# A two-layer conv/attention kernel: the next batch's normalised input staged through DRAM, and the maximum products placed at other points of the score loop

## The reference

```
xn = group_norm(x, 32 groups) * gamma + beta        # per image
q, k, v = split(w_qkv @ xn + b_qkv)                  # 8 heads of 64 channels, 1024 positions
weight = softmax((q*s)^T (k*s), over the keys), s = 64**-0.25
a = weight @ v
out = x + w_proj @ a + b_proj
```

## Time and profile before

| | us |
|---|---|
| median of 3 runs | 2838.94 |
| the runs | 2837.18 to 2839.82 |
| the profiled execution | 2841.34 |
| its span on the core | 2839.8 |
| TensorE matmuls busy | 2620.9 (92%) |
| VectorE busy | 1653.4 (58%) |
| GpSimd busy | 1139.3 (40%) |
| ScalarE busy | 988.6 (35%) |

### The profile page before, as it was taken

The page is one execution under the profiler, slowest core; times in us unless marked ns, Lnnn a source line. Parts: engine busy times, 40 slices in busy tenths (PEclk is TensorE's granted clock), DMA queues, the critical chain, the costliest instruction groups (busy, mean ns, idle before and its releaser), DMA issues.

```text
span 2839.8 us, 38561 instructions
## 1 busy us (share of the span) xinstructions
PE 2620.9 (92%) x13908; PEld 1728.6 (61%) x13908; DVE 1653.4 (58%) x1757; ACT 988.6 (35%) x1215; POOL 1139.3 (40%) x522
## 2 busy tenths in 40 slices
PE   8999999998998999899899989998999899899988
PEld 6888788886554655465447545654655465457544
DVE  5545455455567547745764676367547745764655
ACT  3232222222234323423442343234324423442433
POOL 3320000000264445635661765264445635661762
PEclk9999999998999999999999999999999999999999
DMA  5331111112001110121012011201110121012001
GB/s 182 127 114 40 45 48 44 59 60 96 23 23 39 52 68 23 52 86 42 8 45 104 23 38 45 75 23 40 50 68 23 52 89 39 9 44 104 16 15 60
DMA packets 59262, 155.58 MB, mean 55 GB/s; under 512 B 8704, under 2 KB 8704, under 8 KB 59136
## 3 DMA queue, kind: packets, MB, share of 16 engines
q1 hardware_dynamic: 55552, 141.07, 14.1%
q0 software_dynamic: 3584, 12.58, 1.3%
HBM read 111.69 MB, written 41.94 MB: 54 GB/s over the span
## 4 chain that ended last, share of the span: by engine, by line
PE 79%; DVE 10%; issue 4%; ACT 3%; POOL 3%; DMA 1%; DVEq 0%; ACTq 0%; POOLq 0%; SPq 0%
PE psum L1062 17%; PE psum L1244 13%; PE psum L1293 12%; PE psum L1279 12%; PE psum L1081 6%; PE psum L1254 5%; PE psum L1105 4%; DVE small L901 3%; PE psum L1133 3%; POOL a_all L494 3%; PE psum L1307 2%; DVE r_all L884 2%; PE psum L1176 2%; ACT a_all L648 1%; DVE r_all L892 1%
## 5 line engine op out<-in xcount | busy, mean ns | idle before, releaser
L494 POOL TENSOR_TENSOR a_all<-a_all 128x1024 f32<-128x1024 f32 x441 | 1072.9, 2433 | 1050.0 <-ACT a_all L648 1017.1
L901 DVE TENSOR_REDUCE small<-psum 128x2 f32<-128x1024 f32 x512 | 627.0, 1225 | 426.6 <-PE psum L1254 426.6
L648 ACT ACTIVATE a_all<-psum 128x1024 f32<-128x1024 f32 x512 | 496.1, 1021 | 479.4 <-PE psum L1279 479.4
L1279 PE MATMUL psum<-r_all 64*128 64x512 f32 x4096 | 524.4, 394 | 13.9 <-ACT a_all L648 11.3
L1293 PE MATMUL psum<-a_all 128*64 128x512 f32 x2048 | 499.8, 614 | 9.6 <-ACT a_all L648 7.6
L1062 PE MATMUL psum<-r_all 128*128 128x512 f32 x1920 | 459.2, 400 | 15.6 <-DVE small L901 9.8
L1279 PEld LDWEIGHTS psum<-r_all 64*128 64x128 f32 x4096 | 383.8, 186 | 116.5 <-ACT a_all L648 39.7
L1062 PEld LDWEIGHTS psum<-r_all 128*128 128x128 f32 x1920 | 368.3, 193 | 105.6 <-DVE small L901 12.0
L1244 PE MATMUL psum<-r_all 128*128 128x512 f32 x1536 | 369.2, 396 | 55.9 <-DVE small L901 33.6
L1244 PEld LDWEIGHTS psum<-r_all 128*128 128x128 f32 x1536 | 284.2, 188 | 146.1 <-DVE small L901 37.6
L1254 PE MATMUL psum<-r_all 64*128 64x512 f32 x1024 | 237.7, 459 | 92.2 <-DVE r_all L892 49.1
(11 more groups left out here) (115 smaller groups left out, 1779.4 us busy)
## 6 DMA issues: line engine op xcount, KB each, us to landing
r_all<-w_dram SPq DMA_DIRECT2D x48, 1024.0 KB, 5.1
a_all<-y_dram SPq DMA_DIRECT2D x9, 2048.0 KB, 7.9
a_all<-x SPq DMA_DIRECT2D x16, 1024.0 KB, 6.6
y_dram<-a_all SPq DMA_DIRECT2D x16, 1024.0 KB, 4.2
out<-a_all SPq DMA_DIRECT2D x32, 512.0 KB, 3.0
a_all<-y_dram SPq DMA_DIRECT2D x56, 256.0 KB, 2.7
w_dram<-r_all POOLq DMA_DIRECT2D x16, 512.0 KB, 3.0
a_all<-w POOLq DMA_DIRECT2D x16, 256.0 KB, 3.0
```

Of the source, the lines that this page charges most:

```text
L494: pool.tensor_tensor(p_sum[:, :, cols], probs[:, 0, :, cols] if i == 1 else p_sum[:, :, cols], probs[:, i % SLOTS, :, cols], ALU.add).then ...
L648: act.activation(probs[:, i % SLOTS, :, cols], psum[half][:, :, :], ACT.Exp, scale=SCALE).then_inc(probs_ready, 1)
L901: dve.reduce_max(max2[:, :, tile, half], psum[3][:, :, :], AX_X).then_inc(work_free, 2)
L1279: last = pe.matmul(psum[half][:, h], k[rows_], q[rows_], start=(t == 0), stop=(t == 3))
```

## The change

It does four things. (1) The input of batch b+2 is normalised and split in the tail of batch b (units 0 to 3 beside the V tiles, 4 to 7 beside the projections), stored from a third of `probs` to a DRAM tensor `xn_dram`, and loaded whole into `xn` in one transfer of 4 MB in p = 2 of batch b+1. Batch 1's is staged in the opening phase, beside the first V tiles. ScalarE's queue issues the stores and the later loads of `y_half`. (2) Normalising stands between the reciprocals and behind the last Q/K tile; `hid_lo` follows maxima 0 and 1, and `hid_hi` stands before the last Q/K tile and behind the first exponentials. (3) The maximum products have new places: one behind every score tile, one between the two halves of score tiles 1, 3, 5, 6 and 7, one behind the weighings that follow tiles 1, 3 and 5. None is left before the first score tile or behind the last weighing. (4) Weighings come after the odd score tiles only: 0, then 1 and 2, then 3 and 4, then 5, 6 and 7. The loops over b now end at B - 2, and the last two batches are written out.

```diff
@@ -265,8 +269,13 @@
...
-        NORM_STEP = (1, 2, 3, 3, 4, 5, 5, 6)
-        LO_AT = (4, 6, 8, 9, 10, 12, 13, 14)
+        UNITS = NH * CT
+        EARLY = UNITS // 2
+
+        def unit(u):
+            return u // NH, slice(u % NH * HALF, (u % NH + 1) * HALF)
+
+        MID = (1, 3, 5, NT - 2, NT - 1)
@@ -389,22 +397,25 @@
...
+            load_y(1)
...
-                    load_y(b + 1, range(2))
-                if not last:
-                    load_y(b + 1, range(2, NH * CT))
+                if stage:
+                    load_y(b + 2)
...
                 if not last:
+
+                    for half in xn_stored:
+                        sp.wait_ge(half, (b + 1) * (UNITS // 2) * 16)
+                    sp.dma_start(f(xn), f(xn_dram[b + 1])).then_inc(xn_loaded, 16)
@@ -568,18 +580,36 @@
...
+            def store_xn(tb, u):
+
+                j, cols = unit(u)
+                act.wait_ge(xn_lo_done, tb * UNITS + u + 1)
+                act.dma_start(f(xn_dram[tb, :, :, j, cols]), f(stage_r[:, u % 2])).then_inc(xn_stored[u % 2], 16)
+                if u + 2 < UNITS:
+                    j, cols = unit(u + 2)
+                    act.dma_start(y_half[:, u % 2], y_v[tb, :, j, cols]).then_inc(y_half_loaded[u % 2], 16)
+
+            def norm_unit(tb, u, scale, bias):
+
+                made = (tb - 1) * (UNITS // 2) + u // 2
+                act.wait_ge(y_half_loaded[u % 2], (made + 1) * 16)
+                act.activation(y_half[:, u % 2], y_half[:, u % 2], ACT.Identity, scale=scale(u // NH),
+                               bias=bias(u // NH)).then_inc(xn_made, 1)
+                act.wait_ge(xn_made, tb * UNITS + u + 1)
+                if u >= 2:
+
+                    act.wait_ge(xn_stored[u % 2], made * 16)
+                act.activation(stage_r[:, u % 2, HI], y_half[:, u % 2], ACT.Copy).then_inc(xn_hi_done, 1)
+                if u:
+                    store_xn(tb, u - 1)
+                if u == UNITS - 1:
+                    store_xn(tb, u)
@@ -601,21 +631,24 @@
...
             for i in range(NT):
...
                 act.activation(v_t[:, i], bank(i % CT), ACT.Copy).then_inc(v_first_done, 1)
...
+                norm_unit(1, i, lambda j: xn_scale[:, j, 1:2], lambda j: xn_bias[:, j, 1:2])
...
                     for i in range(QK):
+                        if more and p and i == QK - 1:
+                            hid_hi(b, p - 1, 0)
                         if more:
                             qk_hi((p + 1) % PAIRS, par, i)
@@ -647,16 +684,10 @@
...
                             act.activation(probs[:, i % SLOTS, :, cols], psum[half][:, :, :], ACT.Exp,
                                            scale=SCALE).then_inc(probs_ready, 1)
-                        if p and i in (2, 3):
+                        if p and more and i == 0:
+                            hid_hi(b, p - 1, 1)
+                        if p and not more and i in (2, 3):
                             hid_hi(b, p - 1, i - 2)
-                        if p == 2 and not last:
-                            if i == 1:
-
-                                act.wait_ge(work_full, qk_used(b, 2))
-                                act.wait_ge(next_norm_ready, 2 * b + 2)
-                            for u in range(NH * CT):
-                                if NORM_STEP[u] == i:
-                                    norm_half(b + 1, u)
...
+
+                def stage_units(us_):
+                    for u in us_:
+                        norm_unit(b + 2, u, lambda j: next_norm[:, 0, j:j + 1], lambda j: next_norm[:, 1, j:j + 1])
+
+                if stage:
+
+                    act.wait_ge(sum_step, ONE + (b * PAIRS + PAIRS - 1) * ADDS + 2 * (2 * SLOTS - 1))
+                    act.wait_ge(next_norm_ready, 2 * b + 2)
+                    stage_units(range(EARLY))
                 for h in range(NH):
                     hid_hi(b, PAIRS - 1, h)
@@ -878,10 +922,9 @@
...
-            def norm_lo(b, u):
-                j, cols = u // NH, slice(u % NH * HALF, (u % NH + 1) * HALF)
-                dve.wait_ge(xn_hi_done, b * NH * CT + u + 1)
-                dve.tensor_tensor(xn[:, LO, j, cols], y_half[:, u % 2], f(xn[:, HI, j, cols]), ALU.subtract).then_inc(xn_lo_done, 1)
+            def norm_lo(tb, u):
+                dve.wait_ge(xn_hi_done, tb * UNITS + u + 1)
+                dve.tensor_tensor(stage_r[:, u % 2, LO], y_half[:, u % 2], f(stage_r[:, u % 2, HI]), ALU.subtract).then_inc(xn_lo_done, 1)
@@ -976,9 +1019,11 @@
...
+                if m % 2:
+                    norm_lo(1, m // 2)
             max_join()
@@ -994,36 +1039,27 @@
...
                         invert_sums(pairs - 1, 1)
                     next_qk(2)
                     next_qk(3)
-
-                    def between(m):
-                        if p:
-                            if m in (0, 1):
-                                normalise(pairs - 1, m)
-                            if m in (6, 8):
-                                hid_lo(b, p - 1, (m - 6) // 2)
-                        if p == 1 and m == 4 and not last:
-
-                            dve.wait_ge(xn_hi_done, (b + 1) * NH * CT)
-                            for i, of in enumerate((xn_scale, xn_bias)):
-                                dve.tensor_copy(next_norm[:, i], of[:, :, bass.ds(b + 1, 1)].rearrange("p j a -> p (j a)")).then_inc(next_norm_ready, 1)
-                        if p == 2 and not last:
-                            for u in range(NH * CT):
-                                if LO_AT[u] == m:
-                                    norm_lo(b + 1, u)
+                    if p:
+                        normalise(pairs - 1, 1)
 
                     if more:
                         if p == 0:
                             dve.wait_ge(max_ready, pairs + 1)
                         for m in range(MAXES):
                             max_tile(m)
-                            between(m)
+                            if p and m < NH:
+                                hid_lo(b, p - 1, m)
+                            if p == 1 and m == 4 and stage:
+
+                                dve.wait_ge(xn_hi_done, (b + 2) * UNITS)
+                                for i, of in enumerate((xn_scale, xn_bias)):
+                                    dve.tensor_copy(next_norm[:, i], of[:, :, bass.ds(b + 2, 1)].rearrange("p j a -> p (j a)")).then_inc(next_norm_ready, 1)
                         max_join()
                     else:
-                        for m in range(2):
-                            normalise(pairs - 1, m)
                         for i in range(1, NT):
                             add_last(i, pairs)
                             if i in (4, 5):
@@ -1037,22 +1073,27 @@
...
                         v_tile(b + 1, i)
+                        if stage and i < EARLY:
+                            norm_lo(b + 2, i)
                         if i in (1, 2):
                             invert_sums(pairs, i - 1)
                         if i in (3, 4):
                             normalise(pairs, i - 3)
                         if i in (5, 6):
                             hid_lo(b, PAIRS - 1, i - 5)
-                for o, half in proj_tiles(last):
+                for t, (o, half) in enumerate(proj_tiles(last)):
                     n, ps = work.next()
...
-
-            with dve.Fori(0, B - 1) as b:
...
+                    if stage and 2 <= t < 2 + UNITS - EARLY:
+                        norm_lo(b + 2, EARLY + t - 2)
+
@@ -1264,7 +1305,7 @@
...
-            def scores(pairs, par, i):
+            def scores(pairs, par, i, between):
                 keys = slice(i * P, (i + 1) * P)
@@ -1278,6 +1319,8 @@
...
                     last.then_inc(scores_full, 1)
+                    if half == 0 and i in MID:
+                        between()
@@ -1352,14 +1395,18 @@
...
-                                    pe.wait_ge(xn_lo_done, (b + 2) * NH * CT)
+                                    pe.wait_ge(xn_loaded, (b + 1) * 16)
...
-                    def next_max(m):
+                    made = [0]
+
+                    def next_max():
+                        m = made[0]
+                        made[0] += 1
                         if more:
-                            if m < 2:
-
-                                pe.wait_ge(qk_hi_done, (pairs + 1) * QK + 3 + m)
+                            if m == 0:
+
+                                pe.wait_ge(qk_hi_done, (pairs + 2) * QK)
                             max_tile(1 - par, m)
 
@@ -1368,19 +1415,19 @@
...
-                    next_max(0)
 
                     pe.wait_ge(work_free, turned)
-                    scores(pairs, par, 0)
-                    next_max(1)
-                    for i in range(1, NT):
-                        scores(pairs, par, i)
-                        next_max(2 * i)
-                        weigh(b, p, i - 1)
-                        if i < NT - 1:
-                            next_max(2 * i + 1)
+                    for i in range(NT):
```

(57 more changed lines are left out.)

24 lines of the change are left out of this document (13 added, 11 removed).

## The result

| | before | changed |
|---|---|---|
| median, us | 2839.4 (2837.2 to 2843.7) | 2914.1 (2907.7 to 2919.6) |
| ratio | | 1.0258, interval 1.0235 to 1.0280 |
| the profiled execution | 2841.3 | 2907.7 |
| its span | 2839.8 | 2906.0 |

The change costs 75 us in the medians (four executions of each kernel), 66 in the profiled executions. I had forecast +34, in a range of my own of 2855 to 2895; the wide range, 2836 to 2915, takes the median in by 1 us, at the end that rival D had set. The lines have moved: the maximum product is L1295 now and its reduction L944, scores L1320, weighings L1336, Q/K tiles L1285, V and projection tiles L1103, the addition that evacuates a projection tile L1089; in the staging L602 scales a unit, L927 makes its lower part, L593 stores it and L596 asks for the y of the unit after the next.

The account below looks back on a forecast made before the run. TensorE was taken to bound the kernel, four fifths of the chain of waits. Terms 20 + 27.3 + 7.8 + 19 - 43.4 + 7.5 - 4 gave +34, so 2873 us; own range 2855 to 2895, wide range 2836 to 2915.

Parts of the forecast that it names:

- rival D: Batch tails: the staging chain ends late, last unit some 3.4 us after its bank is wanted; 2908 us, chance 0.12.
- p = 0: +20: First pair of each batch: new order makes the score part 41.0 us instead of 38.5, +2.5 us, 8 times.
- The round of 1.89 us: Score loop: next maximum waits for the reduction, 1.89 us from the last maximum to next work, binding the short gaps.
- rival A: Score loop: the maximum's round is shorter than assumed, so the change is faster; 2814 us at 1.70, chance 0.12.
- The +1.4 of the second lower half: Score loop: hid_lo(1) waits for GpSimd's running addition and delays the fourth maximum, +1.4 us in each of 23 pairs.
- rival B: Score loop: hid_lo(1) slips in ahead of GpSimd's first addition, -1.4 x 23, giving 2841 us; chance 0.08.
- p = 1 and later: Later pairs: p=3 +27.3, last batch's p=1 and p=2 +7.8, other p=1 +19, p=2 without normalising -43.4 us.
- The staging's tail term: Batch tails: a lower part delays a value tile's evacuation 0.5 us, 6 times, +3 us (bounds 0 and 20).
- where I had 4.5: Opening phase: ScalarE and VectorE go at the staging chain's pace from the third unit, +4.5 us (bounds 2 and 17).
- where 7.5 stood: Whole moved staging, opening and tails, with the 4 MB reload hidden: +7.5 us in all.
- 4.8 us a unit: Staging chain: 0.81 to scale, some 0.6 copy, 0.7 for two issues, 2.7 to landing, 4.8 us per unit.
- Rival C: Score loop: short gaps in series lower TensorE's clock, 1.6 us for each of 31 series; 2923 us, chance 0.08.

Follow-up runs that it names:

- run 5: Changed kernel with key tiles weighed singly and a maximum behind every score product and every weighing but the last, only tile 1's halves apart: 2821.7 us, 0.9931.
- run 3: Changed kernel with GpSimd's first addition of a pair waiting until the previous pair's hid_lo is written: 2891.7 us, 1.0196.
- run 9: Changed kernel with the lower parts of units 4 to 7 behind projection tiles 0, 1, 3, 5 instead of 2, 3, 4, 5: 2902.7 us, 1.0214.
- run 7: Changed kernel with each unit's store and the following load issued ahead of the next unit, so two loads are under way: 2909.3 us, 1.0242.
- run 10: Changed kernel with late lower parts behind projection tiles 0, 1, 3, 5, and store and reload issued ahead of the next unit: 2868.8 us, 1.0100.
- run 6: Changed kernel with each load of y issued ahead of the previous unit's store on ScalarE's queue: 2900.5 us, 1.0213.
- run 2: Kernel before with only the new order of maximum products and weighings: 2954.5 us, 1.0420.
- run 1: Changed kernel with the old order of maxima and weighings, keeping the staging and the moved normalising and hid_lo: 2837.8 us, 0.9989.
- run 11: Changed kernel with a maximum behind every score product and weighing but the last, three early and five late units, loads ahead of stores and next unit: 2758.3 us, 0.9702.
- run 12: Old order of maxima and weighings with three early and five late staged units, loads ahead of stores and of the next unit: 2780.3 us, 0.9792.

## Where the prediction held and where it failed

Direction, place and mechanism of the order's cost were right; the sum was 32 us short in the profiled executions, nearly all of it in one term.

**The pairs** came out within 0.8 us of the working. p = 0: +20 on record (54.0 us each), 53.9 to 54.2 us where its first tile ran at full pace. The round of 1.89 us is there and rival A is out (run 5 shows from the other side that the short gaps are the cost: with about 2 us of work between maxima the pair is 51.7). The +1.4 of the second lower half is confirmed by run 3, which takes 1.2 of it away in p = 2 and 3, and rival B is out. This is what the Trainium skill's page "SBUF — State Buffer", section "Who interferes with whom", states of the shared port: a VectorE instruction with two SBUF inputs and a GpSimd instruction that reads SBUF shut each other out. The durations 2.46 beside GpSimd and 0.74 behind the gate agree. p = 1 and later were sized some 0.2 to 0.8 us a pair too high, about 9 us in all.

**The staging's tail term failed.** On record it was 0.5 x 6 = +3, from "the later units end with projection tiles 5 and 6, before the bank is needed". Measured, the six staged tails are 52.2, 52.1, 52.1, 51.2, 51.5 and 49.8 us against 46.8: +28. The first pairs behind them are 2.2 to 3.8 us longer than 54.0, but for the last: +15. The loop's very first pair is +1.5, and the opening window of the earlier trace rows +5.6, where I had 4.5. Together 50 us stand where 7.5 stood, +42; less the 9 us above, that is about the 32 that were missing. Rival D named this mechanism, at 3.4 us a tail and a chance of 0.12; it is 4.7 us a tail and the clock on top.

Three things made the chain slower than 4.8 us a unit. I let a unit start when its inputs were there, and overlooked that unit 6's load hangs on unit 4's lower part, which VectorE's program places behind projection tile 2: it is made 7.5 us after its upper half (995.5 to 1003.0), of which the chain loses some 3, since ScalarE has unit 5 until 1001.0. I took the landing from a trace in which these loads had no stores in their queue, 2.7 us; behind a 512 KB store it is 3.4 to 8.7, median 3.9:
```profile
DMA to landing us min/median/max: 3.4/3.9/8.7
```
And the weights and stores of the result fall into the same stretch. Run 9 shows that the place alone is worth 11 us, run 7 that the second load alone is worth 5 at most, run 10 that both together are worth 45: each cause hides the other. Of the last load's 7.4 us its own queue's store is the smaller part, for with the load ahead of it (run 6, 14 us in all) the load still took 6.5 to 7.8, and with the store ahead of it but the weights behind (run 10) 4.4. The larger part goes with the weights in front of it.

**Rival C**, the clock, was wrong where I had placed it: ten short gaps a pair leave the granted clock at 1.00 (p = 1 to 3 above). The rule of the Trainium skill, "TensorE: Matmul & The Clock Gate", section "A second HAM failure mode: psum-queue depth-cycling", which has the clock swing where TensorE idles briefly between many groups, did not show in these pairs. The rival holds for the long wait ahead of a batch: the stretch behind it is granted 0.96 (0.94 to 0.96 in five of six), and its first tile takes 4.6 to 5.5 us in five of six.

**What the parts are worth.** The new order costs 113 us on the kernel before (run 2) and 76 on the staged one (run 1 against the changed kernel). The staging is worth nothing under the old order as it stands, for its tail eats the 10 us a batch that p = 2 gives back, and 57 us once it is spread.

## What to carry over

Where work is moved into another stage, write down for each transfer which instruction of which engine must be over before it is *issued*, at its place in that engine's program; the chain of these, not the sum of durations, set here when the last unit was done, and also what each transfer ran beside. Two edits that each give little can be two locks on one chain: try them together before ruling either out. And where a buffer's round through two engines takes 1.9 us, put 1.9 us of other work between its uses, or the products between are no cover.

## What the runs showed that I had not expected

The granted clock behind a single wait of TensorE: the first Q/K tile took 3.0 us behind waits up to 1.7 us (run 10) and in all six cases of about 2.0 us in run 11, but 4.6 us in two of the six such cases in run 9 and in three of the six in run 12. Behind 4.3 to 5.7 us it took 4.6 to 5.5 us in the changed kernel, and once, behind 2.85 us, 3.04. In run 6 it took 4.5 us behind 2.53. In the score loop of run 3 it fell behind a single wait of 1.8 us in two cases of six, where ten of 0.5 to 1.2 us a pair left it alone. A first tile at 3.0 us does not mean that the clock held: in run 11 it fell one tile later, behind a second wait of 3.1 to 3.6 us. What decides between cases so alike stays open. A wait of 4.7 us cost some 7 in the changed kernel's batch 1. A 256 KB load behind a 512 KB store in one queue landed after 3.4 to 8.7 us, where one in a queue without stores had taken 2.5 to 5.2.
